# Second attention: attention weights transposed in two row tiles of 64 queries, eight heads at once

## The reference, cut to what matters

```python
scores = jnp.einsum('bhqd,bhkd->bhqk', Qh, Kh) / scale
scores = scores - jnp.max(scores, axis=-1, keepdims=True)
attn = jax.nn.softmax(scores, axis=-1)
attn = jnp.clip(attn, EPS, None)                     # EPS = 1e-12
attn = attn / jnp.sum(attn, axis=-1, keepdims=True)
ctx = jnp.einsum('bhqk,bhkd->bhqd', attn, Vh)
```

## Time and profile before

| | us |
|---|---|
| median of 3 runs | 3350.36 |
| lowest and highest run | 3348.82, 3352.47 |
| profiled execution: span from the first to the last instruction | 3349.9 |
| mean granted PE clock over the span | 0.988 of full speed |
| first and last start of the second attention's transposes (L1679) | 3063.4, 3324.9 |
| length of one round, start of `project_k` (L1643) to the next | 34.5 |
| PE, DVE, ACT busy in a round of 34.46 us | 31.41, 29.59, 31.08 |

### The profile page before, as it was taken

One profiled execution on the slowest core, in us unless ns is written; L12 is line 12 of the kernel. 1 busy time (PEld: TensorE's weight loads), 2 busy tenths in 40 slices (PEclk: granted clock), 3 DMA queues, 4 the chain that ended last, 5 costly groups with the idle time before them and its releaser, 6 DMA issues. The chain is left out here.

```text
span 3349.9 us, 130995 instructions
## 1 busy us (share of the span) xinstructions
PE 3240.1 (97%) x56388; PEld 2053.0 (61%) x56388; DVE 2944.3 (88%) x3353; ACT 2374.4 (71%) x4288; POOL 2640.7 (79%) x1408
## 2 busy tenths in 40 slices
PE   8988999999999999999999999999999999998997
PEld 4555666666666666666666666666666666654554
DVE  6889989999898989999999989898999989975888
ACT  6875677767777677777677767777776777766886
POOL 1229988888888888888888888888888888873667
PEclk9999999999999999999999999999999999999998
DMA  2002433433433443334333334433343343340000
GB/s 96 2 2 65 125 112 109 129 118 114 121 109 116 128 122 116 115 109 129 119 115 119 109 116 126 124 116 111 113 128 118 113 122 109 115 147 26 2 11 18
DMA packets 229205, 336.06 MB, mean 100 GB/s; under 512 B 39062, under 2 KB 151060, under 8 KB 228244
## 3 DMA queue, kind: packets, MB, share of 16 engines
q1 hardware_dynamic: 228628, 327.68, 31.9%
HBM read 124.14 MB, written 102.76 MB: 68 GB/s over the span
## 5 line engine op out<-in xcount | busy, mean ns | idle before, releaser
L828 PE MATMUL psum<-w_qkv,f_xs 128*128 128x512 f32 x2304 | 1078.2, 604 | 11.1 <-DVE f_times_sin L1243 9.5
L1426 POOL TENSOR_TENSOR f_rotated<-f_times_cos,f_times_sin 128x1024 f32<-128x1024 f32 x384 | 909.5, 2369 | 4.2 <-DVE f_times_sin L1243 4.1
L1434 POOL TENSOR_TENSOR f_rotated<-f_rotated,f_rnorm 128x1024 f32<-128x1024 f32 x384 | 723.5, 1905 | 30.3 <-POOL f_rotated L1426 2.2
L828 PEld LDWEIGHTS psum<-w_qkv,f_xs 128*128 128x128 f32 x2304 | 408.7, 191 | 394.0 <-issue 370.3
L1050 ACT ACTIVATE f_squares<-psum 128x1024 f32<-128x1024 f32 x384 | 393.4, 1025 | 338.0 <-PE psum L828 337.1
L1418 POOL TENSOR_TENSOR f_probs<-f_probs,f_rowsum 128x1024 f32<-128x1024 f32 x192 | 365.8, 1905 | 312.9 <-DVE f_rowsum L1284 312.9
L1242 DVE TENSOR_TENSOR f_times_cos<-psum,rot 128x1024 f32<-128x1024 f32 x384 | 469.7, 1223 | 120.1 <-ACT f_squares L1050 115.9
L1070 ACT COPY f_qkT<-psum 128x1024 f32<-128x1024 f32 x384 | 369.7, 1013 | 208.4 <-PE psum L838 208.4
L1243 DVE TENSOR_TENSOR f_times_sin<-psum,rot 128x1024 f32<-128x1024 f32 x384 | 466.1, 1214 | 0.0
L1250 DVE TENSOR_REDUCE f_sumsq<-f_squares 128x16 f32<-128x1024 f32 x384 | 463.5, 1209 | 0.0
L838 PEld LDWEIGHTS psum<-consts,f_rotated 128*128 128x128 f32 x3072 | 349.4, 141 | 89.6 <-issue 79.8
(11 more groups left out here) (178 smaller groups left out, 5166.9 us busy)
## 6 DMA issues: line engine op xcount, KB each, us to landing
f_v_moved<-f_v SPq DMA_DIRECT2D x768, 128.0 KB, 2.8
turned_blocks<-w_qkv SPq DMA_DIRECT2D x192, 512.0 KB, 3.0
f_probsT<-turned_blocks SPq DMA_DIRECT2D x768, 128.0 KB, 2.8
w_qkv<-in_l_wqkv SPq DMA_DIRECT2D x18, 512.0 KB, 4.1
w_o<-in_l_wo SPq DMA_DIRECT2D x6, 512.0 KB, 4.5
w_qkv<-in_ctxT SPq DMA_DIRECT2D x1, 2048.0 KB, 8.7
w<-in_l_w SPq DMA_DIRECT2D x6, 341.0 KB
out<-x_f_result SPq DMA_DIRECT2D x7, 256.0 KB, 2.2
```

The source lines that it names most:

```text
L828: mm = pe.matmul(pairs[i][:, j * BANK:(j + 1) * BANK], xs[g % 2][:, u % GB, :], w_qkv[:, part * INNER + j * BANK:part * INNER + (j + 1) * ...
L1426: pool.tensor_tensor(rotated[u % 2][:, part].rearrange("p h (s d) -> p s h d", s=2), halves(times_cos[part][:, :]), halves(times_sin[part] ...
L1434: pool.tensor_tensor(rt, rt, rnorm[u % 2][:, part * H:(part + 1) * H].unsqueeze(2).broadcast_to([P, H, HD]), ALU.mult).then_inc(normalised ...
```

## The change

`transpose_weights(b, t)` becomes `transpose_weights(b, half)`. For each of eight heads it transposes queries 0 to 63 from partitions 0 to 63 and queries 64 to 127 from partitions 64 to 127, as two row tiles of 64 rows, into two different banks. A bank now holds eight heads of 64 queries instead of four heads of 128. The clip reads one bank as before and writes eight pieces of 64 columns. On PE the two calls of a half stand together, at the place of the first of them; ahead of either, both banks must be free. `ROTATING` follows.

```diff
-            ROTATING = (("t2", 2, 1), ("out", 6, GB), ("mean", -6, GB), ("t3", 2, 1), ("tx", 9, GB), ("mu", 14, GB), ("t0", 1, 1),
-                        ("tq", 13, GB), ("q", -1, GB), ("mix", 2, 1), ("t1", 1, 1), ("k", -3, GB), ("variance", -5, GB),
+            ROTATING = (("t2", 2, 1), ("t3", 2, 1), ("out", 6, GB), ("mean", -6, GB), ("tx", 9, GB), ("mu", 14, GB), ("t0", 1, 1),
+                        ("t1", 1, 1), ("tq", 13, GB), ("q", -1, GB), ("mix", 2, 1), ("k", -3, GB), ("variance", -5, GB),
                         ("v", -2, GB))
...
-                def transpose_weights(b, t):
-                    i = bank_of[f"t{t}", b]
-                    banks.fill(pe, i, (clipped, TURNS * b + t + 1))
-                    pe.wait_ge(normalised[t // 2], b + 1)
-                    for r in range(4):
-                        tr = pe.transpose(psum[:, i, r * S:(r + 1) * S], expo[b % 2][:, 4 * t + r, :], ident)
-                    tr.then_inc(turned, 1)
+                def transpose_weights(b, half):
+                    pair = [2 * half + n for n in range(2)]
+                    for t in pair:
+                        banks.fill(pe, bank_of[f"t{t}", b], (clipped, TURNS * b + t + 1))
+                    pe.wait_ge(normalised[half], b + 1)
+                    for r in range(8):
+                        for n, t in enumerate(pair):
+                            rows = slice(HROWS * n, HROWS * n + HROWS)
+                            tr = pe.transpose(psum[:, bank_of[f"t{t}", b], r * HROWS:(r + 1) * HROWS],
+                                              expo[b % 2][rows, 8 * half + r, :], ident[rows, rows], tile_position=(rows.start, 0))
+                    tr.then_inc(turned, 2)
...
-                    transpose_weights(step - 2, 2)
+                    transpose_weights(step - 2, 1)
                     opening_chunk(project_out)(step - 6)
                     mean(step + 6)
-                    transpose_weights(step - 2, 3)
...
                     mix(step - 2)
-                    transpose_weights(step - 1, 1)
...
-                    dve.tensor_scalar(probsT[b % 2][:, 4 * t:4 * t + 4, :].rearrange("p h n -> p (h n)"), bank(f"t{t}", b), CLIP_EPS, None,
+                    heads, tokens = slice(t // 2 * 8, t // 2 * 8 + 8), slice(t % 2 * HROWS, (t % 2 + 1) * HROWS)
+                    dve.tensor_scalar(probsT[b % 2][:, heads, tokens], bank(f"t{t}", b).rearrange("p (h n) -> p h n", h=8), CLIP_EPS, None,
                                       ALU.max).then_inc(clipped, 1)
```

More of the change, by code:

```diff
@@ L47 @@
 HALFV = INNER // 2
+HROWS = P // 2
 CONSTS = 2 * P + NEAR + 4 * HD + 4
@@ L1768, in pe @@
                     banks.free[i + 1] = banks.free[i]
-                transpose_weights(NB - 2, 2)
-                transpose_weights(NB - 2, 3)
+                transpose_weights(NB - 2, 1)
                 transpose_weights(NB - 1, 0)
                 project_out(7)
-                transpose_weights(NB - 1, 1)
                 transpose_x(6)
                 mix(NB - 2)
-                transpose_weights(NB - 1, 2)
-                transpose_weights(NB - 1, 3)
+                transpose_weights(NB - 1, 1)
                 transpose_x(7)
```

## The result

| | before | changed |
|---|---|---|
| median, us | 3349.59 (4 runs) | 3386.29 (4 runs) |
| lowest and highest run, us | 3342.08, 3352.47 | 3374.92, 3389.66 |
| profiled span, us | 3349.9 | 3373.1 |
| mean granted PE clock over the span | 0.988 | 0.981 |

The ratio is 1.0099, 95% interval 1.0076 to 1.0122: about 33 us slower; the two medians themselves differ by 36.7. The forecast of 3364 us had the sign and the mechanism, and less than half of the size; the time lies above the range. One of ten runs of the kernel before with `project_out` twice, further down, took 13333 us for a reason that the record doesn't show, and is left out of its ratio.

What follows compares the result with a forecast made beforehand. PE, ACT and DVE were taken as near full together, a round being set by waits between them. 3350.4 - 2 (shorter rounds) + 16 (13 added clock falls at 1.2) = 3364 us, range 3346 to 3382.

Steps and rivals of the forecast that it cites:

- 1.2 for each: Second attention: each added fall of PE's clock costs 1.2 us, from 1.4 seen; 13 x 1.2 = +16 us.
- The count: Second attention: about two clock falls a round over the seven later rounds, 14 instead of one.
- the clock that was asked for: Sign in windows over the second attention: granted clock about 0.85; 0.98 or more would mean no slowdown.
- The gaps: PE's idle gaps in a round: 2.25 in M, 0.95 Q, 1.6 and 0.3 N, 1.3 X; 6.4 us instead of 3.06.
- The replay of waits by hand: One round of steps M, Q, N and X followed by its waits, to place PE's gaps and time the round: -0.23 us.
- 0.23 shorter: A round without falls ends 0.23 us early, 34.2 us; seven and a half rounds give -1.7 us.
- Side by side or not: PE's transposes: both row tiles run together, a half of eight heads 0.49 to 0.55 us; 1 us if loads rule.
- the second rival: PE's transposes: weight loads keep the old pace, a half stays 0.98 us; +10 us, 3361, up to 3375; chance 0.13.
- The clip: DVE's clip writing eight pieces of 64 columns: nothing to +0.1 us each, at most +4 us; taken as nothing.
- That the clock holds: Rival: dense mixes and projections keep PE's clock up, fewer than about five falls added; 3348, within 3345 to 3352; chance 0.30.
- many falls: Main case: PE's clock falls often in the second attention, 6 to 22 falls; 3357 to 3384 us; chance 0.47.
- the prediction's own -2 us: Second attention without clock falls: -1.7 us over seven and a half rounds and perhaps -0.5 in the drain.

Runs made afterwards that it cites:

- the run with both of a round gone: Changed kernel with project_out three times in M, variance twice in Q and transposes of x three times in X: 3368.47 us, ratio 1.0043.
- the two runs with one gone: Changed kernel with only project_out three times: 3376.57 us; with only variance twice and transposes of x three times: 3375.63 us.
- the kernels with repeats: Changed kernel with repeated matmuls or transposes in front of its gaps, all or some of them, one with mean later too: 3362.01 to 3376.57 us.
- the run of the order alone: Changed order and ROTATING, with the old full transposes of 128 rows and the clip of the kernel before: 3381.1 us, ratio 1.0092.
- three runs with repeats: Changed kernel with repeats in M, Q and X: 3368.47 us; with second-half transposes also twice: 3362.01; with mean later and repeats: 3362.06.
- experiment with less work in the old order: Kernel before, order and banks untouched, with two of the four transposes of each call left out: 3363.17 us, ratio 1.0035.

## Why the prediction was wrong

**The step that failed is the price of a fall of the clock: "1.2 for each".** The prediction took it from one fall of 3.5 us in the kernel before, scaled down for slack, and let every fall be as short as that one. Seven of the changed kernel's falls last 7 us, and each of these costs 3.0: by the run with both of a round gone (41.0 to 34.98), and by the two runs with one gone (38.0). At 0.52 of the clock, 6.99 us hold 3.6 us of full-clock work, so 3.4 are lost, of which 3.0 are seen. The one fall before lost 1.7 by the same sum, of which 1.4 were seen. For a short fall 1.2 was about right: single ones in the kernels with repeats made rounds of 35.75 to 36.48 out of 35.0, so 0.8 to 1.5 each. What failed is that the length of the falls to come was read off the one that was there.

**The count was right in kind, and not too low.** Two falls a round, in M and N, in each of the last four rounds from one start of `project_k` to the next; the clock that was asked for, about 0.85, was 0.83 to 0.87. The forecast was 14 falls. Behind the long one that reaches into the first round there are ten: three short and seven long. Over all six rounds the windows above give the time at half speed as twice the missing share: 2 x 0.13 x 72.3, 2 x 0.13 x 39.2 and 2 x 0.17 x 123.0, together 71 us, against 5 before. The prediction's 13 added falls of 3.5 us are 46 of these 66 us. The sum of the six rounds, with 3.0 for a long fall and 1.2 for a short one, less the 1.4 of before, is 23.2; half a microsecond a round for the round at full clock makes 26, of the 30 that were lost. The other 4 are in the first two rounds, 3.1 and 0.9 beyond these prices, and the first holds the end of the 17 us fall. That fall starts ahead of the round, and the prediction had no term for it; the run of the order alone doesn't have it (32.54 for its first round), so it may belong to the row tiles, but what makes it is open.

**The gaps held within 0.2 us.** Forecast 2.25, 0.95, 1.6 and 1.3; measured 2.23, 0.75, 1.63 and 1.21. The one of 0.3 ahead of the mix isn't in this round, in which the mix of N lies in the fall; it comes in some rounds of the runs with repeats (0.29 and 0.30) and not in others. The replay of waits by hand was sound, including who ends each: ACT's key biases in M, the wait on the clip in N, ACT's exponentials in Q and X.

**A round at full clock is not 0.23 shorter but some 0.5 longer.** Forecast 34.2, measured 34.98 to 35.04 in three runs with repeats. Part of it is in the rows: `project_q` takes 0.95 to the next start between full transposes and the mix (3191.80 to 3192.75 in the run of the order alone), and 1.06 behind row-tiled ones (3227.18 to 3228.24). The prediction charged a change of tile shape of 0.09 behind `mean` in M and ahead of the bf16 transposes in X, and none between the row-tiled transposes and their 128-row neighbours; a half with its change of shape costs 0.64, not 0.49 to 0.55. Whether this is all of the difference is open. Half a microsecond over six rounds is 3 us, a tenth of the loss.

**Side by side or not.** Forecast 0.49 to 0.55 a half, measured 0.50, and 0.14 for the change of shape, against 0.93 for eight full transposes (3175.46 to 3176.39). So a half did become 0.29 shorter, and the second rival, that the loads keep the old pace, falls. The rule of the Trainium skill (TensorE: Matmul & The Clock Gate, "LDWEIGHTS (loading the stationary operand)") as I had used it put a pair of 128-column loads at no less than 0.11 us; here eight pairs went in 0.50, 0.06 each. The measurement decides: sixteen loads, each recorded with 158 ns, are 2.5 us and went in 0.50 to 0.64, so the recorded loads overlap by more than two at a time. That the two row tiles are what lets them is likely, but no run tells it from a faster load.

**The clip** with eight pieces of 64 columns has 675 ns on average, 674 before: nothing, as taken.

**That the clock holds**, the rival at 0.30, is out: it needed fewer than about five falls added. What spoke for it, "seven of eight rounds before did with 1.39", was also misread: the trace has the gap of 1.39 or 1.38 in five steps M, of which one has the fall, and 0.76 in the first step M of the loop. And it was a sign of how near the edge was and not how far. The experiment with less work in the old order shows it best: its gaps in N are 0.96 and 1.09, where the old kernel has 0.51 and 0.74, and there too the clock fell, with the fall of 17 us beginning between the two.

**The range.** That of "many falls", 3357 to 3384, leaves out the prediction's own -2 us. The measured 3386 lies above it even so, with 22 falls at 1.5.

## What to carry to other kernels

Where PE is not alone in setting the pace and its clock has already been seen to fall, PE time saved can be worth less than nothing, as in the run with half of the transposes left out (ratio 1.0035): it becomes a gap, and behind gaps came stretches at half clock in which ACT and DVE waited for PE. A rare short fall in the kernel before is no price for those that a change adds; let the range reach to falls of twice that length (here 3.0 us each instead of 1.4). Joined calls made a long gap here, and an independent matmul moved into it (41.0 to 38.0 us a round) or repeated in it (41.0 to 38.0 with M filled, 35.0 with all) took the fall away. A run with repeats is a cheap test of whether the clock is what costs. It doesn't price waits: those of the new order, 2.0 us a round by the estimate above, take a run with the order alone.

## What the hardware showed that was not expected

The falls are regular. In the last three rounds of the changed kernel they come at the same two places, 20.5 us apart, and the rounds are alike to 0.05 us: 41.03, 41.00, 40.98. The kernel before had one of 3.5 us behind a gap of 1.39, this one has them of 7 us behind 2.23 and 1.63. What makes a fall long or short was not settled, and the length of the gap ahead of it is not all: the order alone has short falls behind 2.03 and long ones behind 1.44, and in its round of 37.88 none behind 2.03; of the last five gaps of 1.72 with the transposes done twice, three have no fall behind them.

Runs of one kernel can differ by some 10 us, and an early fall is a good part of it. Windows of the first stretch, kernel before, then the one with `project_out` twice in M, whose program is the same up to there:

```profile
20.00:60.00 40.00, 34.76 (x356) 22.29 (x358) 28.29 (x30) 26.20 (x99) 2.98 (x5) 0.83 0.21 61
```

```profile
20.00:60.00 40.00, 34.13 (x416) 22.24 (x422) 32.77 (x35) 30.25 (x119) 3.66 (x7) 1.00 0.22 61
```

The second execution got 60 matmuls further in these 40 us. At 0.83, 40 us lose 6.8 us of full clock; its span is 10 us shorter (3339.7 against 3349.9), though the medians differ by 0.8. So one profile beside one profile tells nothing of 10 us here; rounds have to be compared with rounds.
